# Softmax denominators of the second attention: from a product with ones to block transposes and sums

## The reference

```python
xn = rms_norm(x, gamma)
q, k, v = split(xn @ w_qkv)                  # 16 heads of 64
sim = einsum('bhid,bhjd->bhij', q * 64 ** -0.5, k)
attn = softmax(sim, axis=-1)                 # exp(sim - max) / sum(exp(sim - max))
out = einsum('bhij,bhjd->bhid', attn, v)
out = out.reshape(b, n, 1024) @ w_out
```

## Time and profile before

| What | Value |
|---|---|
| median of 3 runs | 1117.93 us (1117.87 to 1118.39) |
| span of the profiled execution, first to last instruction | 1115.6 us |
| own time of that execution | none beside its span; the median lies 2.3 us above it |
| TensorE busy, granted clock | 1100.7 us (99%), 1.000 |
| VectorE, ScalarE, GpSimd busy | 846.0 (76%), 591.8 (53%), 795.7 us (71%) |
| second attention, steps 0 to 15 | from about 320 to 985 us of the span |

### The profile page before, as it was taken

How to read it: one execution, slowest core, us unless ns; L and a number is a source line. 1 busy time by engine, 2 the same in 40 slices (tenths; PEclk the granted TensorE clock), 3 DMA queues, 4 the chain that set the end, 5 groups by cost and what they waited for, 6 DMA issues and landing times.

```text
span 1115.6 us, 21181 instructions
## 1 busy us (share of the span) xinstructions
PE 1100.7 (99%) x8399; PEld 706.2 (63%) x8399; DVE 846.0 (76%) x1246; ACT 591.8 (53%) x939; POOL 795.7 (71%) x524
## 2 busy tenths in 40 slices
PE   9999999999999999999999999999999999999998
PEld 7899889777755555455455455455455555457886
DVE  4868897666686878878878888888888888896554
ACT  4534334566666555555555455555555555554443
POOL 5778888754367889888888888898889898950000
PEclk9999999999999999999999999999999999999999
DMA  7322223300000002000000000000000000000000
GB/s 251 127 77 80 95 77 115 94 24 1 1 1 1 1 1 105 1 1 1 1 1 1 1 1 1 1 1 1 1 1 1 1 1 1 1 1 10 9 1 19
DMA packets 25601, 30.97 MB, mean 28 GB/s; under 512 B 2064, under 2 KB 21904, under 8 KB 24224
## 3 DMA queue, kind: packets, MB, share of 16 engines
q1 hardware_dynamic: 25184, 29.62, 7.9%
q10 hardware_dynamic: 320, 0.01, 0.0%
HBM read 20.19 MB, written 9.44 MB: 27 GB/s over the span
## 4 chain that ended last, share of the span: by engine, by line
PE 88%; DVE 7%; issue 2%; ACT 2%; POOL 2%; DVEq 0%; POOLq 0%; ACTq 0%
PE o_ps L1713 19%; PE mx_ps L1667 7%; PE st_ps L1697 5%; PE st_ps L1691 5%; PE st_ps L1694 5%; PE ha_banks L647 5%; PE bank L2126 3%; PE bank L2127 3%; PE bank L2128 3%; PE mx_ps L1600 3%; PE pj_ps L1619 2%; PE pj_ps L1611 2%; PE ha_banks L698 2%; PE ha_banks L667 2%; PE ha_banks L709 2%
## 5 line engine op out<-in xcount | busy, mean ns | idle before, releaser
L2040 POOL TENSOR_TENSOR acc<-acc,prob 128x1024 f32<-128x1024 f32 x192 | 468.6, 2440 | 61.9 <-ACT prob L1861 51.7
L1861 ACT ACTIVATE prob<-st_ps 128x1024 f32<-128x1024 f32 x256 | 248.5, 1023 | 206.4 <-PE st_ps L1697 206.3
L1713 PE MATMUL o_ps<-prob,v_cur 128*64 128x512 f32 x1024 | 245.7, 599 | 0.0
L1932 DVE TENSOR_REDUCE mx_part<-mx_ps 128x1 f32<-128x512 f32 x258 | 164.9, 667 | 72.0 <-PE mx_ps L1667 72.0
L1713 PEld LDWEIGHTS o_ps<-prob,v_cur 128*64 128x64 f32 x1024 | 68.1, 136 | 96.2 <-issue 77.5
L1935 DVE TENSOR_REDUCE mx_part<-mx_ps 128x2 f32<-128x1024 f32 x78 | 93.7, 1201 | 44.1 <-PE mx_ps L1667 44.1
L1951 DVE RECIPROCAL rden<-rden 128x128 f32<-128x128 f32 x128 | 120.6, 942 | 0.0
L1667 PEld LDWEIGHTS mx_ps<-k_hi,q_hi 64*128 64x128 f32 x414 | 46.6, 183 | 107.0 <-issue 94.6
L1667 PE MATMUL mx_ps<-k_hi,q_hi 64*128 64x512 f32 x414 | 111.7, 457 | 1.5 <-DVE mx_part L1935 0.8
L1697 PE MATMUL st_ps<-q_hi,d_lo 64*128 64x512 f32 x512 | 100.8, 390 | 0.0
L2040 POOL TENSOR_TENSOR acc<-prob 128x1024 f32<-128x1024 f32 x32 | 76.1, 2378 | 26.2 <-PE pj_ps L1596 18.9
(11 more groups left out here) (419 smaller groups left out, 2349.3 us busy)
## 6 DMA issues: line engine op xcount, KB each, us to landing
v_rows<-ha_v SPq DMA_DIRECT2D x8, 1024.0 KB, 3.9
ha_vt<-v_rows SPq DMA_DIRECT2D x16, 512.0 KB, 4.0
h_w<-in_h SPq DMA_DIRECT2D x2, 1024.0 KB, 8.1
w_raw<-in_w SPq DMA_DIRECT2D x8, 192.0 KB, 3.2
head_wkv<-in_wkv SPq DMA_DIRECT2D x2, 512.0 KB, 6.0
m_w<-in_m SPq DMA_DIRECT2D x3, 256.0 KB, 3.1
out<-fin SPq DMA_DIRECT2D x3, 256.0 KB, 2.3
sel_raw<-in_sel SPq DMA_DIRECT2D x1, 576.0 KB, 11.5
```

The costliest lines, as they stand in the source:

```text
L1713: mm = pe.matmul(o_ps[rows(h), :], v_cur[:, m % 2, j, rows(h)], prob[:, (16 * m + slot) % RING, h, :], start=(j == 0), stop=(j == KT - 1), ...
L1861: act.activation(prob[:, n % RING, :, :], st_ps[:, slot % 2, :, :], ACT.Exp, scale=SCALE).then_inc(s_exp, 1)
L1932: dve.reduce_max(mx_part[:, h, i, keys:keys + 1], maxima_banks(q, n)[h], AX_X).then_inc(s_mxr, 1)
L2040: pool.tensor_tensor(total, old, new, ALU.add).then_inc(s_acc, 1)
```

## The change

The denominators no longer come from a product over 512 columns. When GpSimd has finished `acc` of a half, VectorE transposes it in blocks of 32 x 32 into `rden` (used as scratch), so that each block of 32 queries has its keys along the columns; a reduce sums them to `den_part` (32 columns: 2 heads x 16 blocks). TensorE multiplies by `lanes`, a 0/1 matrix made at the start, which adds up the four groups of 32 partitions and leaves the sums of a head in `pj_ps`, 16 columns wide. VectorE takes the reciprocal of these 16 columns and transposes them back, each column repeated 32 times, into `rden`. ScalarE's copy and the 128-column reciprocals are gone. The units stand in other batches: `den` in 0 and 4, `out` in 2 and 6. VectorE's steps: turn in batches 6 and 2, sum in 7 and 3, reciprocal and turn back in 1 and 5, before the multiplication there. GpSimd's first addition of a half waits for the turn of the step before instead of the product. The tail's order on TensorE and VectorE is written anew.

```diff
@@ -1372,6 +1372,8 @@
     minus = early.sb("minus", [P, P], F32R)
     mx_part = early.sb("mx_part", [P, 2, KT, 2])
     mx_row = early.sb("mx_row", [P, 2, HD])
+    LANES, DEN = 32, CH // 32
+    lanes, den_part, den_rcp = (early.sb(n, [P, size]) for n, size in (("lanes", HD), ("den_part", 2 * DEN), ("den_rcp", DEN)))
     w_hi, w_lo = (pairs.sb(n, [P, PAIRS, W_QK], F32R) for n in ("w_hi", "w_lo"))
 
 
@@ -1402,8 +1404,8 @@
 
     s_mx, s_mxr, s_row, s_max = (at.sem(n) for n in ("s_mx", "s_mxr", "s_row", "s_max"))
 
-    s_v, s_den, s_osum, s_rcp, s_on, s_out = (
-        at.sem(n) for n in ("s_v", "s_den", "s_osum", "s_rcp", "s_on", "s_out"))
+    s_v, s_den, s_osum, s_on, s_out = (
+        at.sem(n) for n in ("s_v", "s_den", "s_osum", "s_on", "s_out"))
 
     s_qhi, s_lo, s_khi, s_kall, s_d = (at.sem(n) for n in ("s_qhi", "s_lo", "s_khi", "s_kall", "s_d"))
     s_qraw = at.sem("s_qraw")
@@ -1412,19 +1414,20 @@
 
     BATCHES = 8
     ADDS = 14
-    RCPS = 4
-
-
-    INVERT = {6: (0, 0, 0), 7: (0, 1, 0), 0: (0, 2, -1), 1: (0, 3, -1),
-              2: (1, 0, -1), 3: (1, 1, -1), 4: (1, 2, -1), 5: (1, 3, -1)}
+    DEN_STEPS = {name: n + 1 for n, name in enumerate(("turned", "summed", "inverse", "back"))}
+
+    def den_done(q, half, name):
+        return len(DEN_STEPS) * (2 * q + half) + DEN_STEPS[name]
+
+    DEN_TURN, DEN_SUM, DEN_BACK = {2: (1, -1), 6: (0, 0)}, {3: (1, -1), 7: (0, 0)}, {1: (0, -1), 5: (1, -1)}
 
     QK = (("qk", 1, 0), ("qk", 0, 0), ("qk", 0, 1), ("qk", 1, 1))
     SLOT_CUT = 12
 
     BEFORE = (QK[0], QK[1], QK[2], ("tr", 1), QK[3], ("v", 0), ("v", 1), ("tr", 0))
-    AFTER = {1: ("den", 1), 3: ("out", 0), 5: ("den", 0), 7: ("out", 1)}
-
-    AHEAD = {**{u: 1 for u in QK}, ("v", 0): 1, ("v", 1): 1, ("tr", 0): 1, ("tr", 1): 0, ("den", 0): 0,
+    AFTER = {0: ("den", 0), 2: ("out", 0), 4: ("den", 1), 6: ("out", 1)}
+
+    AHEAD = {**{u: 1 for u in QK}, ("v", 0): 1, ("v", 1): 1, ("tr", 0): 1, ("tr", 1): 0, ("den", 0): -1,
              ("den", 1): -1, ("out", 0): -1, ("out", 1): -1}
 
     MX = [(i, keys) for first in (0, TT) for keys in range(2) for i in range(first, first + TT)]
@@ -1556,7 +1559,7 @@
         elif u[0] == "v":
             pe.wait_ge(s_v, 2 * q + u[1] + 1)
         elif u[0] == "den":
-            pe.wait_ge(s_den, 2 * q + u[1] + 1)
+            pe.wait_ge(s_den, den_done(q, u[1], "inverse"))
         elif u[0] == "out":
             pe.wait_ge(s_out, 2 * q + u[1] + 1)
         elif u[1] == "var":
@@ -1605,10 +1608,11 @@
                 mm = pe.matmul(to[rows(h), 0:P], mx_row[:, h, :], c.ident[:, :], start=True, stop=True,
                                skip_group_check=True)
         elif u[0] == "den":
-            half = u[1]
-            pe.wait_ge(s_acc, ADDS * q + 7 * (half + 1))
+            if q == 0 and u[1] == 0:
+                pe.wait_ge(s_rowfill, 4)
+            pe.wait_ge(s_den, den_done(q, u[1], "summed"))
             for h in range(2):
-                mm = pe.matmul(pj_ps[rows(h), :], c.ones[:, 0:HD], acc[:, half, h, :],
+                mm = pe.matmul(pj_ps[rows(h), 0:DEN], lanes[:, :], den_part[:, h * DEN:h * DEN + DEN],
                                start=True, stop=True, skip_group_check=True)
         else:
             half = u[1]
@@ -1815,12 +1819,6 @@
             act.wait_ge(s_pj, count_of[q, u])
             act.activation(v_cur[:, q % 2, TT * u[1]:TT * u[1] + TT, :],
                            unit_bank(q, u).rearrange("p (t n) -> p t n", t=TT), ACT.Copy).then_inc(s_v, 1)
-        elif u[0] == "den":
-            half = u[1]
-            if q:
-                act.wait_ge(s_on, 2 * (q - 1) + half + 1)
-            act.wait_ge(s_pj, count_of[q, u])
-            act.activation(rden[:, half, :], pj_ps[:, :], ACT.Copy).then_inc(s_den, 1)
 
     def scalar_differences(act, q):
 
@@ -1883,6 +1881,9 @@
         dve.wait_ge(head.s_yc, head.TURNS)
         dve.memset(mx_row[:, :, :], 0.0).then_inc(s_rowfill, 1)
         dve.memset(mx_part[:, :, :, :], 0.0).then_inc(s_rowfill, 1)
+        for h in range(2):
+            dve.reduce_sum(lanes[:, h * LANES:h * LANES + LANES], c.ident[:, :].rearrange("p (n r) -> p r n", r=LANES), AX_X)\
+               .then_inc(s_rowfill, 1)
 
     def vector_split(dve, p):
         dve.wait_ge(s_whi, p + 1)
@@ -1939,22 +1940,41 @@
             dve.reduce_max(mx_row[:, :, first:first + TT], mx_part[:, :, first:first + TT, :], AX_X)\
                .then_inc(s_row, 1)
 
-    def vector_invert(dve, m, b):
-
-        half, n, ahead = INVERT[b]
-        q = m + ahead
-        if not 0 <= q < STEPS:
-            return
-        if n == 0:
-            dve.wait_ge(s_den, 2 * q + half + 1)
-        part = rden[:, half, tile(n)]
-        dve.reciprocal(part, part).then_inc(s_rcp, 1)
+    def den_at(places, m, b):
+
+        if b not in places:
+            return None
+        half, ahead = places[b]
+        return (m + ahead, half) if 0 <= m + ahead < STEPS else None
+
+    def vector_den_turn(dve, q, half):
+
+        if q or half:
+            dve.wait_ge(s_on, 2 * q + half)
+        dve.wait_ge(s_acc, ADDS * q + 7 * (half + 1))
+        dve.transpose(rden[:, :, :].rearrange("p s n -> p (s n)"), acc[:, half, :, :].rearrange("p h n -> p (h n)"))\
+           .then_inc(s_den, 1)
+
+    def vector_den_sum(dve, q, half):
+        dve.wait_ge(s_den, den_done(q, half, "turned"))
+        if q or half:
+
+            dve.wait_ge(s_pj, count_of[(q, ("den", 0)) if half else (q - 1, ("den", 1))])
+        dve.reduce_sum(den_part[:, :], rden[:, :, :].rearrange("p s (n r) -> p (s n) r", r=LANES), AX_X)\
+           .then_inc(s_den, 1)
+
+    def vector_den_back(dve, q, half):
+        dve.wait_ge(s_pj, count_of[q, ("den", half)])
+        dve.reciprocal(den_rcp[:, :], pj_ps[:, 0:DEN]).then_inc(s_den, 1)
+        dve.wait_ge(s_den, den_done(q, half, "inverse"))
+        dve.transpose(rden[:, half, :].rearrange("p (n r) -> p n r", r=LANES),
+                      den_rcp[:, :].unsqueeze(2).to_broadcast([P, DEN, LANES])).then_inc(s_den, 1)
 
     def vector_normalize(dve, q, half):
         if q:
             dve.wait_ge(s_pj, count_of[q - 1, ("out", half)])
         dve.wait_ge(s_osum, 2 * q + half + 1)
-        dve.wait_ge(s_rcp, RCPS * (2 * q + half + 1))
+        dve.wait_ge(s_den, den_done(q, half, "back"))
         dve.tensor_tensor(o_n[:, half, :], o_sum[:, half, :], rden[:, half, :], ALU.mult).then_inc(s_on, 1)
 
     def vector_begin(dve):
@@ -1984,7 +2004,10 @@
             vector_add_out(dve, *after(*was))
         for name in NORMS_AT.get((m, b), ()):
             e.vector_norm(dve, LAST, name)
-        vector_invert(dve, m, b)
+        if den_at(DEN_BACK, m, b):
+            vector_den_back(dve, *den_at(DEN_BACK, m, b))
+        if den_at(DEN_TURN, m, b):
+            vector_den_turn(dve, *den_at(DEN_TURN, m, b))
         at_b = before(m, b)
         if second:
             vector_maxima(dve, *second)
@@ -1992,6 +2015,8 @@
             vector_spread_max(dve, *at_b)
         if at_b and at_b[1][0] == "qk":
             vector_low(dve, *at_b)
+        if den_at(DEN_SUM, m, b):
+            vector_den_sum(dve, *den_at(DEN_SUM, m, b))
         if b == 1 and m >= 1:
             vector_normalize(dve, m - 1, 0)
         if b == 5 and m >= 1:
@@ -2032,7 +2057,7 @@
         if j == 1:
             old = prob[:, (16 * m + slot - 1) % RING, :, :]
             if m:
-                pool.wait_ge(s_pj, count_of[m - 1, ("den", half)])
+                pool.wait_ge(s_den, den_done(m - 1, half, "turned"))
         else:
             old = total
             pool.wait_ge(s_acc, ADDS * m + 7 * half + j - 1)
@@ -2455,14 +2480,14 @@
                 for m in range(HT):
                     end.tensor_first(pe, 0, m)
 
-                t2.tensor(pe, STEPS, 1)
+                t2.tensor(pe, STEPS, 2)
                 end.tensor_hidden(pe, 0, 1, 0)
                 end.tensor_hidden(pe, 0, 1, 1)
-                t2.tensor(pe, STEPS, 3)
+                t2.tensor(pe, STEPS, 4)
                 end.tensor_hidden(pe, 0, 1, 2)
                 end.tensor_hidden(pe, 0, 1, 3)
                 end.tensor_hidden(pe, 0, 2, 0)
-                t2.tensor(pe, STEPS, 7)
+                t2.tensor(pe, STEPS, 6)
                 for k in range(CHUNKS):
                     if k:
                         for m in range(HT):
@@ -2548,18 +2573,17 @@
                 for m in range(HT):
                     end.vector_first(dve, 0, m)
                 t2.vector(dve, STEPS, 1)
+                t2.vector(dve, STEPS, 2)
                 end.vector_x(dve, 1)
+                t2.vector(dve, STEPS, 3)
 
                 end.vector_hidden(dve, 0, 1, 0)
-                t2.vector(dve, STEPS, 2)
-                t2.vector(dve, STEPS, 3)
                 end.vector_hidden(dve, 0, 1, 1)
-                t2.vector(dve, STEPS, 4)
+                t2.vector(dve, STEPS, 5)
                 end.vector_hidden(dve, 0, 1, 2)
-                t2.vector(dve, STEPS, 5)
```

(2 more changed lines are left out.)

## The result

The changed kernel takes 1155.47 us (median of 4 runs, 1154.9 to 1157.14) against 1118.16 us (median of 4) beside it. The ratio is 1.0337, 95% interval [1.0322, 1.0352]. The forecast was 1155 us. The profiled span is 1152.7 us, 37.1 us longer than before.

The account below looks back on a forecast made before the run. TensorE was taken as the bound. To 1117.9 us it added 36.3 for fourteen steps, 1.35 for step 15, -0.85 for step 0 and 1.5 for the tail: 1156, stated as 1155, range 1140 to 1170 us (chance 0.64).

Parts of the forecast that it names:

- Bound: TensorE, busy for 99% of the span, has no stall to give back; only work removed or waits added move the end.
- The waits at batches 3 and 7: Second maxima product waits for the output's addition on VectorE, starting at T + 2.78 us; batch length 5.28 us.
- S: Start of a batch's second maxima product on TensorE; without a wait 1.72 us after T.
- T: Start of a batch, its first maxima product on TensorE; VectorE can start on those maxima 0.54 us later.
- The waits at batches 1 and 5: Second maxima product waits for the 16-column reciprocal, starting at T + 2.15 us; length 5.34 us, not 4.81.
- Batches 0 and 4: New product waits 0.40 and 0.07 us for VectorE's projection read; late sum adds 0.15; lengths 5.98 and 5.65 us.
- The small product: TensorE's 16-column product replacing the denominator's 0.85 us: taken as 0.17 us, bounds 0.05 and 0.44.
- VectorE's prices: Transpose 1.2, sum 1.2, reciprocal 0.25, transpose back 0.68 us; together 3.3 against 3.8 us per half-step.
- Rival 1: VectorE's transposes are slow or held, at 2.40 us, delaying batches 2 and 6: 22 us more, 1177 us; chance 0.14.
- The tail: First half's last output now precedes the last network's first hidden product: +1.5 us, bounds -1 and +5.
- rival 2: Bank waits stay under 0.68 us per half-step, so the removed product wins; 1096 us without waits; chance 0.07 below 1116.
- Rival 3: A small loss: signals 0.05 us, refills nothing, projection's read earlier; 1125 to 1140 us; chance 0.12.

Follow-up runs that it names:

- turn_late: The changed kernel with one more 1024-column reduce, its result overwritten, ahead of the transpose in batches 2 and 6; 1176.71 us.
- add_first: The changed kernel with the output's addition issued on VectorE ahead of the first maxima's reduces; 1127.43 us.
- place: The kernel before, with its old denominators, and only the output unit moved from batches 3 and 7 to 2 and 6; 1149.11 us.
- rcp_first: The changed kernel with the 16-column reciprocal issued ahead of the first maxima's reduces in batches 1 and 5; 1141.73 us.
- out_37: The changed kernel with the output unit back in batches 3 and 7, the tail's calls moved along; 1121.97 us.
- tail: The changed kernel with the last step's first output put behind the first two hidden products, VectorE's part likewise; 1149.40 us.
- rcp_first_37: The changed kernel with the output back in batches 3 and 7, the reciprocal ahead of the first maxima's reduces, and the tail's order rearranged; 1102.40 us.

## Why the prediction was right, point by point

**Bound.** TensorE's chain without stalls: shown for the second attention. Taking the two bank waits out shortened steps 1 to 14 by 41.5 us, where 26 and 15 were expected for the whole, and a longer VectorE step moved the end only by the part that reached TensorE (turn_late).

**The waits at batches 3 and 7.** S at T + 2.77 (2.78 forecast), length 5.35 (5.28). The way from S to the next T took 2.58 us where the forecast had 2.50: the two reduces ahead of the maxima's spreading took 1.20 us (735.82 to 737.02) instead of 1.13. Shown as cause by add_first (-28.0 us) and, without the new denominators, by place (+30.8 us).

**The waits at batches 1 and 5.** S at T + 2.15 as forecast, length 5.34 and 5.32 (5.34). Shown by rcp_first.

**Batches 0 and 4.** The product waits for the projection's read and starts in batch 0 at S + 3.41 (761.82 to 765.23; 3.40 forecast). The late first reduce, for which I set 0.15 us, does not move S: in batch 4 it is at T + 2.17 (737.85 to 740.02), where it was at T + 2.18 before, though VectorE did start late (sum at 737.62). It costs less, and behind S. The reduce that frees the bank ends at 739.97, so the product at S gets its weights only at 740.01, where before the change they were loaded 0.22 us ahead of it (721.43 for 721.65). Its record has 0.50 us, and the unit follows after 0.43 us (740.02 to 740.45) instead of 0.32. In out_37, where nothing delays that reduce, the same place reads

```profile
720.27 0.40 PE L1671 MATMUL mx_ps<-k_hi,q_hi 64*128 64x512 f32 x2
720.60 0.50 PE L1597 MATMUL pj_ps<-xr_hi,w_hi 128*128 128x512 f32 x1
...
723.26 0.28 PE L1615 MATMUL pj_ps<-den_part,lanes 128*64 128x16 f32 x4
```

and the small product comes 2.99 us behind S, not 3.09. Batches 0 and 4 have 5.71 and 5.38 us there, and 5.81 and 5.47 here, where 5.98 and 5.65 stood in the forecast: 0.10 us each for the late reduce. The 0.33 us a step by which the sum was too large are 0.35 in these two batches and 0.10 in batch 2, which L1978 did not cost (5.66), less 0.07 each in batches 3 and 7; the rest is rounding.

**The small product.** 0.21 us from start to start (743.11 to 743.32). The products with v took 0.09 us longer in front of a maxima product (1.86 us, 722.87 to 724.73 in the trace of before) than in front of the denominators' (1.77, 706.81 to 708.58), and that is no longer paid at their end. So the addition is about 0.12 us. I had 0.17.

**VectorE's prices.** Turn, sum, reciprocal and turn back: 1.23, 1.21, 0.25 and 0.71 us against 1.2, 1.2, 0.25 and 0.68. Rival 1 did not come true, and turn_late shows its price, 21 us for 22 forecast.

**The tail was mis-sized.** Forecast +1.5 us. From T of batch 3 in step 15 to the last output product the time grew by 4.5 us (961.94 to 1008.16 before, 994.53 to 1045.21 after). TensorE's timeline there, and the windows (us, busy of each engine, granted clock third from the right):

```profile
1021.58 0.39 PE L2153 MATMUL bank<-x_lo,m_hi 128*128 128x512 f32 x1
1027.33 1.98 PE L1623 MATMUL pj_ps<-o_n,wo 128*64 128x512 f32 x4 [5.36 <-DVE o_n L1978]
1029.23 0.80 PE L2151 MATMUL bank<-act00hi,h_hi 128*128 128x512 f32 x1
...
1031.96 0.56 PE L2151 MATMUL bank<-act02hi,h_hi 128*128 128x512 f32 x1
```

```profile
1022.00:1026.00 4.00, 0.00 (x0) 0.00 (x0) 3.88 (x8) 2.60 (x4) 2.12 (x4) 0.94 0.00 0
...
1028.00:1032.00 4.00, 4.00 (x11) 2.19 (x8) 3.19 (x5) 0.00 (x0) 0.00 (x0) 0.50 0.00 0
1032.00:1036.00 4.00, 4.00 (x18) 3.30 (x17) 1.12 (x2) 0.69 (x1) 0.00 (x0) 0.96 0.01 4
```

TensorE stands still for 5.36 us before the output. The forecast's own time for `o_n`, 994.0 with 0.15 for the signal, against the end of the record before it (990.46 in the trace of before), makes 3.7. VectorE was not as early as I worked out. Measured from the last product of the first network's block, it starts on act03lo 0.8 us earlier than before (1024.75 less 1021.58, against 994.07 less 990.07), not 2.4. It waited 3.66 and then 0.62 us for results of ScalarE, and act00lo, with two inputs in SBUF while GpSimd was adding, took 2.02 us where before it took 0.92. Behind the gap the granted clock is 0.50, the lower of the two levels, and the products are slower until 1031.96. The output (1027.33 to 1029.23) takes 1.90 us instead of 1.01, and the six products from 1029.23 to 1031.96 take 2.73 us instead of 1.5 (one of 0.34 and five of 0.23): about 2.1 us for the clock. The sum had no term for that. Gap and clock are 7.5 us; the stretch grew by only 4.5, in the main because one output (0.99 us) and the old denominators' products are no longer in it. The Trainium skill, "TensorE: Matmul & The Clock Gate", section "What's actually happening", describes a clock that is granted by recent activity. This trace agrees, with 0.50 behind the gap, and so does tail, where without the gap it stays at the upper level (1.00 from 1020 to 1040 us).

**The nearness of the total is partly luck.** The steps came out some 4 us shorter than forecast (32.6 against 36.8 us at T of batch 3 in step 15), the tail 3 us longer. The rivals: 2 is refuted for this order, since the waits did bite. Once they are gone, as in rcp_first_37 (which has the new order in the tail too), the smaller product does win, 15.4 us. But it wins less than the 0.68 us a half-step on which rival 2 stands: a step has 40.63 us against 41.65, 0.51 a half-step. Batches 1 and 5 give back 0.85 us each; batches 0 and 4 take 0.47 and 0.13 of it for the small product and the wait for the projection's read, and batch 2 takes 0.09. Rival 3, shorter signals and no refills, did not show: S stood at T + 2.15 and T + 2.77.

## What to carry to other kernels

When a unit that borrows a shared PSUM bank is moved, list who takes that bank next and where, in the reading engine's queue, the read stands: its time from the batch's start, not the engine's total load, is the price. Put a read of a bank whose data are ready ahead of work whose data are still being made; here that alone was worth 41.8 us. After work is moved to another engine, read the hand-written ends of the program for themselves: here a single gap there cost 5.4 us, more than any one wait in the loop, and about 2.1 us more by the clock after it.

## What the runs showed of the hardware

VectorE's block transposes of float32 were not held by GpSimd here. Their rows over the whole span, in which GpSimd is busy for 69% (min/median/max ns), beside the multiplication with two SBUF inputs:

```profile
L1955 DVE STREAM_TRANSPOSE rden<-acc x32: 1212/1234/1245, 356.0 to 1027.2; 128x1024 f32<-128x1024 f32 x32
```

```profile
L1970 DVE STREAM_TRANSPOSE rden<-den_rcp x32: 711/711/714, 371.6 to 1038.6; 128x512 f32<-128x512 f32 x32
```

```profile
L1978 DVE TENSOR_TENSOR o_n<-o_sum,rden x32: 681/1064/1831, 374.4 to 1039.4; 128x512 f32<-128x512 f32 x32
```

Of the 32 transposes of 1024 columns, 31 ran in part or wholly while GpSimd was at work, and took 1212 to 1236 ns; the one that did not took 1245. Those of 512 columns took 711 to 714 ns. The multiplication took 681 to 1831 ns.

The two sizes differ by 1.02 ns a column, and a fixed 0.19 us remains; this is an estimate, since the narrower transpose also has another input, each column repeated 32 times. No plain transpose of 512 columns was run, so what the repetition costs is not shown; it can't be much, as the whole took 0.03 us more than a copy of that size out of PSUM (711 against 681 ns, L1926). The Trainium skill, "Vector Engine (DVE) Microarchitecture Reference", section "3.8 The reshape front-end and per-opcode configuration", says that the TRANSPOSE mode sustains one element per cycle per lane. No run here shows the cycle itself, but the trace agrees in that a transpose of 1024 columns took 1.23 us where a reduce that reads as many took 1.21.
